# State product of the first attention's chunks: 64x64 matmuls on two quarters of the array for three of four query groups

## What is computed

```python
def step(carry, inp):                 # one token, 16 query heads, k and v of 64 features
    Hkk, Hkv = carry
    qt, kt, vt, gt = inp
    d = jnp.exp(gt)[..., None, None]
    Hkk = d * Hkk + kt[..., :, None] * kt[..., None, :]
    Hkv = d * Hkv + kt[..., :, None] * vt[..., None, :]
    xq = qt
    for _ in range(2):
        xq = qt - 0.25 * jnp.einsum('bhk,bhkl->bhl', xq, Hkk)
    ot = jnp.einsum('bhk,bhkv->bhv', xq, Hkv)
```

## Time and profile before

| | |
|---|---|
| median of 3 runs | 2659.98 us |
| all runs | 2660.24, 2659.98, 2646.7 us |
| profiled execution, its own time | 2658.76 us |
| span of the profile, first to last instruction | 2656.9 us |
| time outside of the span | 1.9 us |
| PE busy | 2371.1 us, 89% of the span |
| PE weight loads busy | 1219.7 us |
| DVE, ACT, POOL busy | 1639.1, 1458.3, 782.5 us |
| mean granted TensorE clock | 0.952 |
| chunks of the first attention | about 202 to 619 us of the span |

### The profile page before, as it was taken

One profiled execution on the slowest core, in us unless ns is written; L12 is line 12 of the kernel. 1 busy time (PEld: TensorE's weight loads), 2 busy tenths in 40 slices (PEclk: granted clock), 3 DMA queues, 4 the chain that ended last, 5 costly groups with the idle time before them and its releaser, 6 DMA issues. The chain is left out here.

```text
span 2656.9 us, 41487 instructions
## 1 busy us (share of the span) xinstructions
PE 2371.1 (89%) x13315; PEld 1219.7 (46%) x13402; DVE 1639.1 (62%) x2942; ACT 1458.3 (55%) x3263; POOL 782.5 (29%) x830
## 2 busy tenths in 40 slices
PE   7978999998797789999999998978998759998878
PEld 3445666665586222222222225874444544443333
DVE  5777988975332789999999842332445522444555
ACT  3572333333465478888888886655444337553344
POOL 1224665640233600000000002343543024442113
PEclk9988999998899799999999999998999879998899
DMA  5343223211375321021111003867666018665112
GB/s 163 87 145 121 86 92 107 90 37 42 110 215 158 91 31 32 10 41 20 24 26 16 4 5 122 275 197 269 225 216 208 1 58 308 220 202 141 27 31 74
DMA packets 206358, 287.34 MB, mean 108 GB/s; under 512 B 25168, under 2 KB 129104, under 8 KB 203408
## 3 DMA queue, kind: packets, MB, share of 16 engines
q1 hardware_dynamic: 187752, 234.80, 29.6%
q0 software_dynamic: 18432, 50.36, 6.1%
HBM read 176.04 MB, written 107.73 MB: 107 GB/s over the span
## 5 line engine op out<-in xcount | busy, mean ns | idle before, releaser
L3264 DVE TENSOR_REDUCE big<-psum 128x2 f32<-128x1024 f32 x512 | 602.6, 1220 | 70.5 <-PE psum L3052 68.3
L3216 ACT ACTIVATE probs<-psum 128x512 f32<-128x512 f32 x1024 | 554.8, 598 | 120.0 <-PE psum L3079 111.9
L3079 PE MATMUL psum<-big,k_ops 128*128 128x512 bf16 x946 | 291.8, 387 | 13.1 <-ACT probs L3216 11.0
L1735 PE MATMUL psum<-big,turned 128*128 x480 | 234.1, 616 | 16.8 <-ACT turned L1895 13.0
L1834 PE MATMUL psum<-big,probs 128*128 128x512 f32 x512 | 231.6, 603 | 6.1 <-DVE down_sum L2015 6.1
L3079 PEld LDWEIGHTS psum<-big,k_ops 128*128 128x128 bf16 x1024 | 80.8, 97 | 328.2 <-ACT probs L3216 258.2
L1429 ACT ACTIVATE hidden<-psum,big 128x128 f32<-128x128 f32 x480 | 136.2, 372 | 98.9 <-PE psum L1322 98.4
L644 POOL DMA_INDIRECT linear_rows<-desk_tokens,linear_row x128 | 124.6, 974 | 208.0 <-DVE linear_row L620 105.4
L1685 POOL DMA_INDIRECT big<-linear_y,linear_row x128 | 124.8, 975 | 203.8 <-PE psum L1735 128.6
L1903 ACT ACTIVATE big<-psum 128x512 f32<-128x512 f32 x240 | 139.9, 597 | 78.6 <-PE psum L1735 67.2
L3052 PE MATMUL psum<-big,w_A_or_L_A 32*128 32x512 bf16 x1024 | 159.9, 391 | 23.5 <-DVE big L3264 15.8
(11 more groups left out here) (505 smaller groups left out, 4004.5 us busy)
## 6 DMA issues: line engine op xcount, KB each, us to landing
linear_y<-big SPq DMA_DIRECT2D x240, 256.0 KB, 4.1
big<-in_experts SPq DMA_DIRECT2D x120, 322.0 KB, 3.9
big<-step_rows SPq DMA_DIRECT2D x16, 1024.0 KB, 4.7
qkv_chunks<-big SPq DMA_DIRECT2D x48, 256.0 KB, 2.3
big<-qkv_chunks SPq DMA_DIRECT2D x16, 768.0 KB, 4.5
big<-linear_rows SPq DMA_DIRECT2D x48, 256.0 KB, 3.9
big<-since_rows SPq DMA_DIRECT2D x32, 256.0 KB, 5.4
big<-row_store SPq DMA_DIRECT2D x32, 256.0 KB, 5.3
```

Source lines behind the costliest of these rows:

```text
L1735: pe.matmul(k.bank[bank_of(n, m)][:, :], turned[:, q % 2, t % 4, :], w["up" if r else "gate"][:, bass.ds(experts[r][t] * TB, TB)], start=T ...
L3079: pe.matmul(ring_bank(ring_at(i, m))[:, :], k_ops[:, g % 2, h, kt * P:(kt + 1) * P], q_ops[:, g % 2, i % QB, h, :], start=True, stop=True) ...
L3216: act.activation(probs[:, kt % 2, h, :], ring_bank(ring_at(i, m))[:, :], ACT.Exp, scale=SCALE).then_inc(expd.sem, 1)
L3264: dve.tensor_reduce(into, k.row_pair[hp].rearrange("p (h t) -> p h t", h=2), AX.X, ALU.max).then_inc(row_max.sem, 1)
```

## The change

The matmul of group r = 0 stays as it is. For r = 1, 2 and 3 the one 128x128 matmul becomes two 64x64 matmuls: the lower diagonal block of the state with rows 0 to 63 of `x_since` into partitions 0 to 63 of the bank, and the upper block with rows 64 to 127 into partitions 64 to 127. The zero blocks are no longer multiplied. For each pair and step, 4 matmuls become 7. All waits and increments stay where they were; `x_used` is now incremented by the last 64x64 matmul.

```diff
                     pe.wait_ge(since_ready.sem, since_ready.at(c * 6 + (2 * u + p)))
-                    for r in range(R):
-                        mm = pe.matmul(k.bank[4 + p][:, r * CH:(r + 1) * CH],
-                                       state[b][:, p, r, 0:2, :].rearrange("q h f -> q (h f)"),
-                                       x_since[:, p, r, :], start=(r == 0), stop=False)
+                    pe.matmul(k.bank[4 + p][:, 0:CH], state[b][:, p, 0, 0:2, :].rearrange("q h f -> q (h f)"), x_since[:, p, 0, :],
+                              start=True, stop=False)
+                    for r in range(1, R):
+                        for half, rows in enumerate(halves):
+                            mm = pe.matmul(k.bank[4 + p][rows, r * CH:(r + 1) * CH], state[b][rows, p, r, half, :],
+                                           x_since[rows, p, r, :], start=False, stop=False)
                     mm.then_inc(x_used.sem, 1)
```

## The result

| | before | after |
|---|---|---|
| median of 11 runs each | 2657.5 us | 2667.16 us |
| profiled execution, its own time | 2658.76 us | 2670.98 us |
| span of the profile | 2656.9 us | 2669.1 us |
| mean granted TensorE clock | 0.952 | 0.951 |
| one chunk of the loop | 24.78 us | 25.56 us |

After over before is 1.0042, with a 95% interval of 1.0029 to 1.0055: slower by about 11 us (the two medians alone lie 9.7 us apart). The profiled execution is longer by 12.2 us. Predicted were 2671.4 us for that execution and a chunk of 25.58 us.

What follows compares the result with a forecast made beforehand. PE was taken to bound each chunk; 13 chunks at + 0.80 us gave 10.4, and chunks 0, 1 and 15 0.7, 1.2 and 0.33: + 12.6 us on 2658.76, so 2671.4 us. The range given was 2656 to 2692 us.

Steps and rivals of the forecast that it cites:

- The bound: In the chunk loop, PE is busy for all 24.78 us, so each chunk lasts as long as PE's list of work.
- The slot: In groups 1 to 3, two quarters take 0.109 us in place of 0.112, saving at most 0.018 us per pair and product.
- rival of quarters that don't run together: In the state products, two quarters run one after the other: 41 us more, 2712 us; chance 0.10.
- the unhidden load: In the quarters, the weight load is not hidden, 0.160 us a slot: 19 us more, 2691 us; chance 0.05.
- The change of shape: On PE, entering or leaving 64x64 costs as the nearest rows do, 0.144 or 0.206 us; three more changes per product.
- rival without shape cost: In the state products, quarters follow the full array freely: 1 us less, 2658 us; chance 0.07.
- The product and the wait: Each product gains 0.470 us; in u=0 PE's 0.142 us wait for ACT absorbs part, leaving 0.328; a chunk gains 0.80.
- The ends of the stage: Outside chunks 2 to 14: chunk 0 gains 0.7 us, chunk 1 1.2, chunk 15 0.33, its u=1 hidden by waiting for DVE.
- The sum: Over the stage, 10.4 + 0.7 + 1.2 + 0.33 = 12.6 us more, so 2671.4 us for the profiled execution.
- The clock: From 250 to 600 us the clock stays at 1.00; rival: idle array lowers it, + 35 us, 2706; chance 0.04.
- The chances: For the whole program: faster by over 0.5% 0.03, within 0.5% 0.44, slower by over 0.5% 0.53.

Runs made afterwards that it cites:

- column halves: Kernel before with each 128x128 state product as two 128x64 matmuls, zero blocks still multiplied: 24.22 us a chunk, program 2644.06 us, ratio 0.9958.
- one group in quarters: Changed kernel with only group 3 in 64x64 quarters, groups 0 to 2 on the full array: 25.60 us a chunk, one run 2669.56 us.
- step 1 only: Changed kernel with product(u=0) as before and only product(u=1) in quarters: 25.24 us a chunk, one run 2650.08 us.

## Why the prediction was right, point by point

- **The bound.** PE was busy for all of a chunk before and after. Right. The prediction counts 12 changes of shape in a chunk of before; the trace has 13 (19 after). No term of the sum uses that count.
- **The slot.** 0.109 us for two quarters, as taken from the column halves (unrounded that quotient is 0.1097); 0.110 measured. The reason given for the gain, the zeros left out, is not what shortens it: the column halves multiply the zeros and have the same slot. The rival of quarters that don't run together (2712 us) and that of the unhidden load (2691 us) have fallen with it: 12 records in 0.87 us leave room for neither. The Trainium skill, TensorEngine Tiling (Array Packing), Gotcha 1: PSUM Pressure, says that two row tiles cannot access one PSUM bank at the same time. The quarters of the change write one bank, on different partitions and from different column halves, their matmuls start 0.007 us apart, and they take one slot together; for two row tiles on the same columns no run here shows it.
- **The change of shape.** No row of before had a quarter; the bounds were 0 and 0.144 to 0.206. It costs what the nearest rows cost: 0.20 from matmul to load both ways, and 0.46 net for the three of product(u=1). The rival without shape cost (2658 us) has fallen, and "one group in quarters" shows it apart from the quarters themselves. The rule of the Trainium skill, TensorEngine Tiling (Array Packing), Key Properties, that a change of mode drains TensorE, agrees with the 0.20 us at every change to and from 64x64 here; that a drain fills this time no row shows.
- **The product and the wait.** u=1 + 0.460 (0.470 predicted), u=0 + 0.323 (0.328): a chunk + 0.782 (0.80). The wait of 0.142 in u=0 was given its due place; "step 1 only" separates the two.
- **The ends of the stage.** Here lies the miss. Chunk 0: from product(u=0) to the scores of step 2 12.37 us before and 13.03 after, + 0.66 against 0.7. Chunk 15 hides u=1: the wait for DVE at the second part of the product shrinks from 4.69 to 4.23 us; its u=0 cost 0.44 instead of 0.33, since before it had no wait for ScalarE to give (2.01 us, not 2.12). Chunk 1 was mis-sized: + 2.0 us, with 1.2 predicted. Product(u=0) took 4.45 us instead of 3.34, and the part at L3835 2.34 instead of 1.87, because the half clock, which before rose during this product, now lasted beyond it. The clock rose at about 239.5 us before and 242.1 after; the prediction let the clock rise where it had risen before.
- **The sum.** 12.6 us predicted, + 12.2 in the profiled execution, and that this is so near is in part luck. The stage itself got 13.3 us longer from chunk 0's first product to chunk 15's second: 0.66 in chunk 0, 2.05 in chunk 1, 10.2 in the 13 chunks behind it (0.782 each), 0.44 in chunk 15. But it began 0.67 us earlier than before (201.52 against 202.19), which lies ahead of the changed lines and which no run explains, so the last product's second part begins 12.65 us later (611.37 against 598.71). By the end of the stage 11.1 are left: the half clock there lasted 6.8 us before and 3.4 after, so that this part took 4.33 us before and 3.62 after, and the norm behind it 1.96 and 1.16. The stages behind add 1.1.
- **The clock.** 1.00 from 250 to 600 us, as before. The rival has fallen.
- **The chances.** The ratio lies within 0.5%, on which I had put 0.44, with 0.53 on slower by more. The sum stood 0.7 us below that line, and 1.0042 is 11.2 us, 1.4 below the sum; the interval reaches over the line, so the runs don't decide between the two.

## What to carry to other kernels

Before cutting a matmul to the part of the array that holds data, look at what fills its slot: with 128 moving columns the slot was 0.11 us on the full array, on two halves and on two quarters alike. Quarters without the zeros were no faster than column halves with them, and both only 0.002 us a slot faster than the full array. Count the changes of shape in the order on PE instead: each cost 0.14 to 0.21 us here, so the shape to choose is that of the neighbours, even with more instructions and more zeros (0.9958). Then look which wait the saved time runs into, for a change of shape that covers a wait costs that much less (0.14 us here).

## What the runs showed of the hardware beyond that

- Quarters that are not neighbours in the program overlap in part: six records of one half followed by six of the other took 7.5 steps of 0.109 us, not 11, and the second series began right behind the third start of the first.
- A change of shape between float32 matmuls has a steady price. In every kernel of this case, in the stage of the chunks and where nothing else was waited for, the load behind a change stood 0.196 to 0.204 us behind the start of a last matmul of 128 moving columns at the full clock, and 0.35 us behind it at half clock, whatever the two shapes were; behind one of 512 columns it was 0.52. For the bfloat16 matmuls of another stage (L3065 to L3052, from 128x128 to 32x128) it was 0.15 us with 128 columns.
- A single time of the program said the opposite of its own profile: 2650.08 us for a kernel whose loop is 0.46 us a chunk slower than before (14 chunks, 6.4 us), with a mean granted clock of 0.955 where before had 0.952.
